# Another order for the steps of the first batch in a fused attention and gated-FFN kernel

## The chip, the cores and the metric

One NeuronCore of a Trainium2 chip runs the whole program. The metric is the device time of one execution in microseconds, the median of the runs.

## The reference

The input x has 16 batches of 512 tokens with 256 channels, float32. Each batch goes through self-attention with 16 heads of 16 channels and a causal mask, a residual and a layer norm, and then a gated FFN of hidden size 1024 with scaled weights, again with residual and layer norm:

```python
qkv = x @ Wqkv + bqkv
att = softmax(where(causal, q @ k.T * scale, -inf))
x = layernorm(x + (att @ v) @ Wout + bout)
h = silu((x @ w1.T) * s1) * ((x @ w2.T) * s2)
h = gelu((h @ h1.T) * sh1)
h = gelu((h @ h2.T) * sh2)
x = layernorm(x + (h @ w3.T) * s3)
```

## The kernel before

Each engine runs its own program, and all of them walk through the same written lists of steps, each picking out its own share of a step. `HEAD_ORDER` (line 116) is the list of the first iteration: the attention of batch 0, the first part of batch 1's attention, and the loading and testing of the FFN's weights. `FIRST_ORDER` (line 145) follows it, then `ORDER` (line 62), the loop in which one batch's attention runs beside the FFN of the batches before, and `TAIL_ORDER`. A step's name has the kind, the batch (0 or 1 in the head) and its arguments: `max:1:0:3:2` is the row maximum of batch 1, group 0, token tile 3, head 2. The 16 heads are worked in four groups of four.

The steps that matter here:

- `qk` (PE line 1170): a group's queries and keys. ACT writes the high half of the sum with the bias (line 796), DVE the low half (line 931). For batch 0 the halves lie in buffers of their own; for batch 1 they all go through the one buffer `c`, so ACT waits until the group before has been saved (line 792). SP saves the halves to DRAM in four transfers (lines 528 to 531).
- `stack`: the operands of the scores. In batch 0 PE sets them out with pick matrices (lines 1122 and 1127) and ACT copies them (lines 737 and 740). In batch 1 SP loads them in six transfers (lines 592 to 595) when the save has landed.
- `max`: PE makes scores (line 1110), DVE takes the row maximum (line 915), two banks in turn. `neg_split` (lines 923 and 925) negates a group's maxima and splits them, `neg_max` turns them on PE (line 1136), and ACT copies them into the stack (line 774). The group's exponentials wait for that.
- `exp`: PE makes the transposed scores (line 1098), ACT the exponential (line 765), GpSimd the causal mask (line 682). A group has eleven. `pv` is the product with V (line 1158), `o_out` its copy by ACT (line 816) and its move by SP (lines 616 and 617).
- `v`: a tile of V (PE line 1190, ACT line 804). `bias` is the output bias (line 1177); GpSimd adds it to the input rows, which `load_x` has SP load (lines 562 and 697).
- `raw` and `weights`: ACT issues two transfers for each of eleven pieces of the FFN's weights, DRAM to DRAM (line 744), and from there to SBUF when that has landed (line 748). `weight_test` has DVE gather the low bits of a piece (line 899), `low_bits` reduces them (line 903), and `weight_flag` (lines 906 and 1182) makes a flag of them. PE loads the flag and takes one of two copies of the rest of the program (line 1272).
- `den`, `rec_save`, `rec_load`, `den_turn`, `y`, `ln1_stats`, `ln1` and `x1_turn`: the division by the softmax's sums, the output projection, the layer norm and the turn of batch 0 for the FFN.

The order on an engine is that of the list; nothing is moved at run time. A step of which an engine has no share is skipped by it. The PSUM ring of three banks is given out by the list too (`ring_banks`, line 206): a step waits until the one before it in its bank has been read.

Of the kernel before, what the change touches and what calls it, by code (L numbers as in the profile page):

```python
# [113 lines left out]


HEAD_ORDER = """
raw:0:0 qk:0:0 qk:0:1 stack:0:0 max:0:0:3:0 table:0:Exp:0 max:0:0:3:1 stack:0:1 columns:0 raw:0:1 max:0:0:3:2
max:0:0:3:3 qk:0:2 max:0:0:2:0 max:0:0:2:1 v:0:0 raw:0:2 max:0:0:2:2 max:0:0:2:3 max:0:0:1:0 qk:0:3
max:0:0:1:1 max:0:0:1:2 stack:0:2 max:0:0:1:3 raw:0:3 max:0:0:0:0 max:0:0:0:1 stack:0:3 max:0:0:0:2
max:0:0:0:3 weights:0:0 neg_split:0:0 v:0:1 load_x:0 max:0:1:3:0 max:0:1:3:1 raw:0:4 v:0:2 max:0:1:3:2  # L120
max:0:1:3:3 neg_max:0:0 bias:0 exp:0:0:0 exp:0:0:1 max:0:1:2:0 weights:0:1 v:0:3 max:0:1:2:1 exp:0:0:2
max:0:1:2:2 exp:0:0:3 max:0:1:2:3 exp:0:0:4 max:0:1:1:0 exp:0:0:5 raw:0:5 max:0:1:1:1 exp:0:0:6 max:0:1:1:2
pv:0:0:0 weights:0:2 max:0:1:1:3 exp:0:0:7 max:0:1:0:0 exp:0:0:8 exp:0:0:9 max:0:1:0:1 max:0:1:0:2 weights:0:3
max:0:1:0:3 exp:0:0:10 raw:0:6 neg_split:0:1 max:0:2:3:0 max:0:2:3:1 neg_max:0:1 load_xT:1 pv:0:0:1
max:0:2:3:2 o_out:0:0 max:0:2:3:3 exp:0:1:0 weights:0:4 max:0:2:2:0 exp:0:1:1 max:0:2:2:1 exp:0:1:2
max:0:2:2:2 raw:0:7 exp:0:1:3 max:0:2:2:3 exp:0:1:4 max:0:2:1:0 raw:0:8 exp:0:1:5 max:0:2:1:1 exp:0:1:6
max:0:2:1:2 pv:0:1:0 max:0:2:1:3 weights:0:5 exp:0:1:7 max:0:2:0:0 exp:0:1:8 max:0:2:0:1 exp:0:1:9 max:0:2:0:2
exp:0:1:10 raw:0:9 max:0:2:0:3 neg_split:0:2 max:0:3:3:0 pv:0:1:1 o_out:0:1 qk:1:0 max:0:3:3:1 raw:0:10
neg_max:0:2 max:0:3:3:2 max:0:3:3:3 exp:0:2:0 max:0:3:2:0 stack:1:0 exp:0:2:1 weights:0:6 max:0:3:2:1
exp:0:2:2 max:0:3:2:2 exp:0:2:3 max:0:3:2:3 exp:0:2:4 max:0:3:1:0 weights:0:7 exp:0:2:5 max:0:3:1:1 exp:0:2:6  # L130
weights:0:8 max:0:3:1:2 pv:0:2:0 max:0:3:1:3 exp:0:2:7 exp:0:2:8 max:0:3:0:0 max:0:3:0:1 exp:0:2:9 max:0:3:0:2
exp:0:2:10 max:0:3:0:3 neg_split:0:3 qk:1:1 weights:0:9 weights:0:10 weight_test:0:0 neg_max:0:3 max:1:0:3:0
pv:0:2:1 o_out:0:2 stack:1:1 weight_test:0:1 weight_test:0:2 exp:0:3:0 exp:0:3:1 max:1:0:3:1 exp:0:3:2
exp:0:3:3 exp:0:3:4 weight_test:0:3 max:1:0:3:2 weight_test:0:4 exp:0:3:5 exp:0:3:6 max:1:0:3:3 pv:0:3:0
exp:0:3:7 max:1:0:2:0 exp:0:3:8 weight_test:0:5 exp:0:3:9 max:1:0:2:1 exp:0:3:10 pv:0:3:1 weight_test:0:6
o_out:0:3 den:0 max:1:0:2:2 v:1:0 v:1:1 weight_test:0:7 max:1:0:2:3 max:1:0:1:0 weight_test:0:8 max:1:0:1:1
max:1:0:1:2 max:1:0:1:3 weight_test:0:9 max:1:0:0:0 max:1:0:0:1 max:1:0:0:2 max:1:0:0:3 neg_split:1:0
weight_test:0:10 v:1:2 low_bits:0 neg_max:1:0 rec_save:0 rec_load:0 exp:1:0:0 max:1:1:3:0 exp:1:0:1
max:1:1:3:1 exp:1:0:2 max:1:1:3:2 exp:1:0:3 exp:1:0:4 max:1:1:3:3 max:1:1:2:0 exp:1:0:5 exp:1:0:6 v:1:3
exp:1:0:7 max:1:1:2:1 exp:1:0:8 max:1:1:2:2 exp:1:0:9 max:1:1:2:3 exp:1:0:10 den_turn:0 qk:1:2 y:0:0:0  # L140
max:1:1:1:0 o_out:1:0 max:1:1:1:1 y:0:0:1 y:0:1:0 y:0:1:1 ln1_stats:0 max:1:1:1:2 max:1:1:1:3 pv:1:0:1 ln1:0
stack:1:2 max:1:1:0:0 max:1:1:0:1 max:1:1:0:2 max:1:1:0:3 neg_split:1:1 x1_turn:0:0 neg_max:1:1 x1_turn:0:1
"""
# [1171 lines left out]
```

## Time and profile before

| | |
|---|---|
| median of 3 runs | 2251.17 us (2250.86 to 2251.55) |
| span of the profiled execution | 2245.9 us |
| PE busy | 2155.0 us, 96% |
| DVE busy | 1266.2 us, 56% |
| ACT busy | 1314.8 us, 59% |
| GpSimd busy | 490.6 us, 22% |
| mean granted PE clock | 0.986 of full speed |

The span runs from the first to the last instruction of the one profiled execution; that execution has no time of its own beside it, and what the runs have over it lies around the span. A line of a timeline reads: start in us, duration in us, engine, line of the kernel, operation, output and inputs, count, and in brackets the idle time before it with what ended it. SPq and ACTq are the queues on which SP and ACT issue transfers. PEld is the load of PE's stationary operand, whose time lies beside PE's.

### The profile page before, as it was taken

What the parts mean: (1) busy time and instruction counts of PE and PEld (TensorE: products, weight loads), DVE (VectorE), ACT (ScalarE), POOL (GpSimd) and SP (SyncE); (2) the same over time, 40 slices, a digit from 0 to 9 for tenths busy, and PEclk for the clock granted to TensorE, in tenths of its full rate; (3) what the DMA queues carried; (4) which work ended last, traced back from release to release, by engine and by line L of the source; (5) the groups of instructions that cost most, each with busy time, mean ns of one, the idle gap of its engine ahead of it and who ended that gap; (6) DMA issues with size and microseconds to landing.
All of it is one profiled execution on the core that took longest, in us unless ns stands there. A gap on an engine that the chain in (4) does not pass through costs nothing.

```text
span 2245.9 us, 52053 instructions
## 1 busy us (share of the span) xinstructions
PE 2155.0 (96%) x16294; PEld 1874.6 (83%) x16294; DVE 1266.2 (56%) x3928; ACT 1314.8 (59%) x2807; POOL 490.6 (22%) x899
## 2 busy tenths in 40 slices
PE   7679999999999999999999999999999999999998
PEld 4348888888888889888888888889888888888898
DVE  6664655655555565555655565565555655555452
ACT  5446565665656666565665666566565665655553
POOL 2212222221221222122221222222122221221220
PEclk9869999999999999999999999999999999999999
DMA  7823232222322223232223323223232223322100
GB/s 254 277 66 73 56 72 66 71 68 69 83 62 68 71 69 77 65 77 71 61 70 79 74 54 74 65 65 77 65 78 68 62 69 80 77 51 52 32 6 10
DMA packets 95942, 167.72 MB, mean 75 GB/s; under 512 B 19204, under 2 KB 38404, under 8 KB 95672
## 3 DMA queue, kind: packets, MB, share of 16 engines
q1 hardware_dynamic: 88152, 141.22, 25.4%
q10 hardware_dynamic: 7520, 23.07, 2.9%
q8 instruction: 149, 2.44, 0.5%
q14 instruction: 121, 0.99, 0.2%
HBM read 98.26 MB, written 68.17 MB: 74 GB/s over the span
## 4 chain that ended last, share of the span: by engine, by line
PE 65%; issue 14%; DVE 3%; ACT 3%; DMA 3%; POOL 3%; SPq 2%; ACTq 0%; DVEq 0%; POOLq 0%
PE ring L1235 35%; PE ring L1220 7%; PE pO L1158 5%; PE pS L1098 4%; PE pM L1110 4%; PE ring L1170 4%; PE ring L1248 3%; DMA qk_d<-c 2%; POOL Xlo L689 2%; PE ring L1200 1%; ACT c L796 1%; DVE c L931 1%; ACT probs_b L765 1%; DVE full_g L954 1%; DVE x1Tlo L939 1%
## 5 line engine op out<-in xcount | busy, mean ns | idle before, releaser
L915 DVE CUSTOM_DVE_ANT_0 pM<-pM,mask 128x512 f32<-128x512 f32 (+3 forms) x1024 | 494.7, 505 | 350.2 <-PE pM L1110 281.2
L1235 PE MATMUL ring<-Yhi,H 128*128 128x256 f32 x1984 | 495.3, 286 | 6.1 <-DVE c L931 5.9
L1235 PE MATMUL ring<-Xhi,H 128*128 128x256 f32 x1984 | 497.6, 290 | 0.0
L1235 PE MATMUL ring<-Ylo,H 128*128 128x256 f32 x1984 | 487.9, 282 | 0.0
L1235 PE MATMUL ring<-Xlo,H 128*128 128x256 f32 x1984 | 483.8, 283 | 0.0
L1235 PEld LDWEIGHTS ring<-Yhi,H 128*128 128x128 f32 x1984 | 378.2, 191 | 16.0 <-issue 9.5
L1235 PEld LDWEIGHTS ring<-Xhi,H 128*128 128x128 f32 x1984 | 379.0, 191 | 4.5 <-issue 3.4
L1235 PEld LDWEIGHTS ring<-Ylo,H 128*128 128x128 f32 x1984 | 379.0, 191 | 3.3
L1235 PEld LDWEIGHTS ring<-Xlo,H 128*128 128x128 f32 x1984 | 379.8, 191 | 1.1
L1110 PE MATMUL pM<-Ks,Qs 128*128 128x512 f32 x992 | 287.2, 341 | 24.9 <-DVE mx L915 12.7
L859 ACT ACTIVATE Yhi<-ring,cols 128x256 fp32r<-128x256 f32 x248 | 117.4, 474 | 292.1 <-PE ring L1235 227.6
L1098 PE MATMUL pS<-Qs,Ks 128*128 128x512 f32 x744 | 258.1, 394 | 22.6 <-ACT probs_b L765 6.9
L1220 PE MATMUL ring<-x1Thi,W 128*128 128x256 f32 x1024 | 255.1, 285 | 5.6 <-DVE full_g L954 3.8
L1220 PE MATMUL ring<-x1Tlo,W 128*128 128x256 f32 x1024 | 252.9, 282 | 0.0
L860 ACT ACTIVATE full_h<-ring,cols 128x256 f32<-128x256 f32 x512 | 239.0, 467 | 0.0
L859 ACT ACTIVATE Xhi<-ring,cols 128x256 fp32r<-128x256 f32 x248 | 117.2, 472 | 187.1 <-PE ring L1235 141.5
L1110 PEld LDWEIGHTS pM<-Ks,Qs 128*128 128x128 f32 x992 | 172.3, 192 | 49.1 <-DVE mx L915 21.7
L682 POOL TENSOR_SCALAR_AFFINE_SELECT probs_a<-probs_a 128x256 f32<-128x256 f32 x144 | 62.4, 435 | 667.6 <-ACT probs_a L765 667.1
L1220 PEld LDWEIGHTS ring<-x1Thi,W 128*128 128x128 f32 x1024 | 194.6, 190 | 12.7 <-issue 5.8
L962 DVE TENSOR_TENSOR Xlo<-full_h,Xhi 128x256 fp32r<-128x256 f32 x248 | 113.0, 456 | 157.5 <-ACT full_h L860 156.1
L1098 PEld LDWEIGHTS pS<-Qs,Ks 128*128 128x128 f32 x744 | 133.3, 191 | 78.7 <-ACT probs_b L765 27.4
L1220 PEld LDWEIGHTS ring<-x1Tlo,W 128*128 128x128 f32 x1024 | 194.8, 190 | 2.8
(148 smaller groups left out, 3554.5 us busy)
## 6 DMA issues: line engine op xcount, KB each, us to landing
qk_d<-c SPq DMA_DIRECT2D x120, 256.0 KB, 3.4
Qs<-qk_d SPq DMA_DIRECT2D x120, 192.0 KB
Ks<-qk_d SPq DMA_DIRECT2D x120, 192.0 KB
qk_d<-c SPq DMA_DIRECT2D x120, 128.0 KB, 3.1
xTs<-in_xT SPq DMA_DIRECT2D x16, 512.0 KB, 4.9
xz<-in_x SPq DMA_DIRECT2D x16, 512.0 KB, 4.0
raw<-in_h ACTq DMA_DIRECT2D x8, 1024.0 KB, 8.8
H<-raw ACTq DMA_DIRECT2D x8, 1024.0 KB, 13.6
```

The lines of the kernel that those rows point to most:

```text
L682: nc.gpsimd.affine_select(out=tri_p, in_=tri_p, compare_op=ALU.is_ge, fill=0.0, base=0, pattern=[[0, 2], [1, P]], channel_multiplier=-1).t ...
L859: nc.scalar.activation(hi, src, ACT.Gelu, scale=sc)
L860: nc.scalar.activation(full_h[:], src, ACT.Gelu, scale=sc).then_inc(h_full, 1)
L915: nc.vector.tensor_tensor_reduce(pM[:, h % 2, 0:n], pM[:, h % 2, 0:n], mask[:, T - n:T], 1.0, NEG, ALU.add, ALU.max, mx[:, t, h:h + 1]).th ...
L962: nc.vector.tensor_tensor(lo[:, j], full_h[:], hi[:, j].bitcast(F32), ALU.subtract).then_inc(h_lo, 1)
L1098: mm = nc.tensor.matmul(pS[:, nth % 2, n * wide[0]:n * (wide[-1] + 1)], K[:, p, kt * P:(kt + 1) * P], Q[:, p, first:last + 1, kt * P:T], s ...
L1110: nc.tensor.matmul(pM[:, h % 2, 0:n], Q[:, h // 2, h % 2, t * P:(t + 1) * P], K[:, h // 2, 0:n], start=True, stop=True).then_inc(m_ready, 1)
L1158: mm = nc.tensor.matmul(pO[32 * j:32 * j + VW, kt * P:T], Vo[:, kt, G * g + j], probs_of(steps, off, g, kt)[:, p, s, 0:n], start=(kt == 0) ...
L1170: mm = nc.tensor.matmul(to, Wqk[:, c, g], xTs[:, c], start=(c == 0), stop=(c == CB - 1))
L1220: mm = nc.tensor.matmul(to[:, n * HALF:(n + 1) * HALF], w, x_part, start=(c == 0 and X is x1Thi), stop=(c == CB - 1 and X is x1Tlo))
L1235: mm = nc.tensor.matmul(to, w, x_part, start=(k == 0 and m == 0), stop=(k == KB - 1 and m == 1))
L1248: mm = nc.tensor.matmul(to[:, t * C:(t + 1) * C], x_part, w, start=(k == 0 and m == 0), stop=(k == KB - 1 and m == 1))
```

## The change

The list of the first iteration is written in another order. The set of its 250 steps is the same, and so is everything outside the list. Among other moves, the input rows and the bias come earlier; the projection and stack of group 3 and three of batch 0's V tiles come behind the first group's maxima; the first two projections and stacks of batch 1 come about one group of batch 0 earlier; the weights' first pieces are issued earlier and the last two later; the first weight tests come between the last maxima of batch 0, the last ones beside the second group of batch 1; the reduction of the low bits comes near the end.

```diff
--- before.py
+++ after.py
@@ -114,32 +114,32 @@
 
 
 HEAD_ORDER = """
-raw:0:0 qk:0:0 qk:0:1 stack:0:0 max:0:0:3:0 table:0:Exp:0 max:0:0:3:1 stack:0:1 columns:0 raw:0:1 max:0:0:3:2
-max:0:0:3:3 qk:0:2 max:0:0:2:0 max:0:0:2:1 v:0:0 raw:0:2 max:0:0:2:2 max:0:0:2:3 max:0:0:1:0 qk:0:3
-max:0:0:1:1 max:0:0:1:2 stack:0:2 max:0:0:1:3 raw:0:3 max:0:0:0:0 max:0:0:0:1 stack:0:3 max:0:0:0:2
-max:0:0:0:3 weights:0:0 neg_split:0:0 v:0:1 load_x:0 max:0:1:3:0 max:0:1:3:1 raw:0:4 v:0:2 max:0:1:3:2
-max:0:1:3:3 neg_max:0:0 bias:0 exp:0:0:0 exp:0:0:1 max:0:1:2:0 weights:0:1 v:0:3 max:0:1:2:1 exp:0:0:2
-max:0:1:2:2 exp:0:0:3 max:0:1:2:3 exp:0:0:4 max:0:1:1:0 exp:0:0:5 raw:0:5 max:0:1:1:1 exp:0:0:6 max:0:1:1:2
-pv:0:0:0 weights:0:2 max:0:1:1:3 exp:0:0:7 max:0:1:0:0 exp:0:0:8 exp:0:0:9 max:0:1:0:1 max:0:1:0:2 weights:0:3
-max:0:1:0:3 exp:0:0:10 raw:0:6 neg_split:0:1 max:0:2:3:0 max:0:2:3:1 neg_max:0:1 load_xT:1 pv:0:0:1
-max:0:2:3:2 o_out:0:0 max:0:2:3:3 exp:0:1:0 weights:0:4 max:0:2:2:0 exp:0:1:1 max:0:2:2:1 exp:0:1:2
-max:0:2:2:2 raw:0:7 exp:0:1:3 max:0:2:2:3 exp:0:1:4 max:0:2:1:0 raw:0:8 exp:0:1:5 max:0:2:1:1 exp:0:1:6
-max:0:2:1:2 pv:0:1:0 max:0:2:1:3 weights:0:5 exp:0:1:7 max:0:2:0:0 exp:0:1:8 max:0:2:0:1 exp:0:1:9 max:0:2:0:2
-exp:0:1:10 raw:0:9 max:0:2:0:3 neg_split:0:2 max:0:3:3:0 pv:0:1:1 o_out:0:1 qk:1:0 max:0:3:3:1 raw:0:10
-neg_max:0:2 max:0:3:3:2 max:0:3:3:3 exp:0:2:0 max:0:3:2:0 stack:1:0 exp:0:2:1 weights:0:6 max:0:3:2:1
-exp:0:2:2 max:0:3:2:2 exp:0:2:3 max:0:3:2:3 exp:0:2:4 max:0:3:1:0 weights:0:7 exp:0:2:5 max:0:3:1:1 exp:0:2:6
-weights:0:8 max:0:3:1:2 pv:0:2:0 max:0:3:1:3 exp:0:2:7 exp:0:2:8 max:0:3:0:0 max:0:3:0:1 exp:0:2:9 max:0:3:0:2
-exp:0:2:10 max:0:3:0:3 neg_split:0:3 qk:1:1 weights:0:9 weights:0:10 weight_test:0:0 neg_max:0:3 max:1:0:3:0
-pv:0:2:1 o_out:0:2 stack:1:1 weight_test:0:1 weight_test:0:2 exp:0:3:0 exp:0:3:1 max:1:0:3:1 exp:0:3:2
-exp:0:3:3 exp:0:3:4 weight_test:0:3 max:1:0:3:2 weight_test:0:4 exp:0:3:5 exp:0:3:6 max:1:0:3:3 pv:0:3:0
-exp:0:3:7 max:1:0:2:0 exp:0:3:8 weight_test:0:5 exp:0:3:9 max:1:0:2:1 exp:0:3:10 pv:0:3:1 weight_test:0:6
-o_out:0:3 den:0 max:1:0:2:2 v:1:0 v:1:1 weight_test:0:7 max:1:0:2:3 max:1:0:1:0 weight_test:0:8 max:1:0:1:1
-max:1:0:1:2 max:1:0:1:3 weight_test:0:9 max:1:0:0:0 max:1:0:0:1 max:1:0:0:2 max:1:0:0:3 neg_split:1:0
-weight_test:0:10 v:1:2 low_bits:0 neg_max:1:0 rec_save:0 rec_load:0 exp:1:0:0 max:1:1:3:0 exp:1:0:1
-max:1:1:3:1 exp:1:0:2 max:1:1:3:2 exp:1:0:3 exp:1:0:4 max:1:1:3:3 max:1:1:2:0 exp:1:0:5 exp:1:0:6 v:1:3
-exp:1:0:7 max:1:1:2:1 exp:1:0:8 max:1:1:2:2 exp:1:0:9 max:1:1:2:3 exp:1:0:10 den_turn:0 qk:1:2 y:0:0:0
-max:1:1:1:0 o_out:1:0 max:1:1:1:1 y:0:0:1 y:0:1:0 y:0:1:1 ln1_stats:0 max:1:1:1:2 max:1:1:1:3 pv:1:0:1 ln1:0
-stack:1:2 max:1:1:0:0 max:1:1:0:1 max:1:1:0:2 max:1:1:0:3 neg_split:1:1 x1_turn:0:0 neg_max:1:1 x1_turn:0:1
+raw:0:0 qk:0:0 raw:0:1 load_x:0 qk:0:1 stack:0:0 max:0:0:3:0 max:0:0:3:1 weights:0:0 v:0:0 raw:0:2 max:0:0:3:2
+max:0:0:3:3 stack:0:1 columns:0 qk:0:2 max:0:0:2:0 max:0:0:2:1 max:0:0:2:2 max:0:0:2:3 raw:0:3 max:0:0:1:0
+stack:0:2 bias:0 max:0:0:1:1 weights:0:1 max:0:0:1:2 max:0:0:1:3 max:0:0:0:0 max:0:0:0:1 max:0:0:0:2 max:0:0:0:3
+neg_split:0:0 max:0:1:3:0 raw:0:4 neg_max:0:0 max:0:1:3:1 qk:0:3 stack:0:3 raw:0:5 max:0:1:3:2 max:0:1:3:3
+weights:0:2 max:0:1:2:0 weights:0:3 v:0:1 max:0:1:2:1 v:0:2 v:0:3 max:0:1:2:2 max:0:1:2:3 max:0:1:1:0
+max:0:1:1:1 exp:0:0:0 exp:0:0:1 max:0:1:1:2 max:0:1:1:3 exp:0:0:2 exp:0:0:3 exp:0:0:4 max:0:1:0:0 exp:0:0:5
+exp:0:0:6 exp:0:0:7 max:0:1:0:1 max:0:1:0:2 exp:0:0:8 pv:0:0:0 max:0:1:0:3 exp:0:0:9 exp:0:0:10 neg_split:0:1
+table:0:Exp:0 neg_max:0:1 raw:0:6 load_xT:1 max:0:2:3:0 max:0:2:3:1 pv:0:0:1 max:0:2:3:2 max:0:2:3:3 exp:0:1:0
+max:0:2:2:0 exp:0:1:1 max:0:2:2:1 exp:0:1:2 max:0:2:2:2 exp:0:1:3 max:0:2:2:3 exp:0:1:4 max:0:2:1:0 exp:0:1:5
+max:0:2:1:1 weights:0:4 max:0:2:1:2 o_out:0:0 max:0:2:1:3 max:0:2:0:0 exp:0:1:6 qk:1:0 raw:0:7 max:0:2:0:1
+pv:0:1:0 exp:0:1:7 exp:0:1:8 exp:0:1:9 stack:1:0 max:0:2:0:2 max:0:2:0:3 exp:0:1:10 raw:0:8 weights:0:5
+neg_split:0:2 neg_max:0:2 qk:1:1 stack:1:1 o_out:0:1 raw:0:9 pv:0:1:1 max:0:3:3:0 max:0:3:3:1 exp:0:2:0
+max:0:3:3:2 exp:0:2:1 exp:0:2:2 max:0:3:3:3 exp:0:2:3 max:0:3:2:0 exp:0:2:4 exp:0:2:5 max:0:3:2:1 weights:0:6
+max:0:3:2:2 max:0:3:2:3 exp:0:2:6 weights:0:7 max:0:3:1:0 max:0:3:1:1 max:0:3:1:2 exp:0:2:7 exp:0:2:8
+max:0:3:1:3 max:0:3:0:0 pv:0:2:0 max:0:3:0:1 exp:0:2:9 weights:0:8 max:0:3:0:2 weight_test:0:0 exp:0:2:10
+max:0:3:0:3 weight_test:0:1 raw:0:10 neg_split:0:3 neg_max:0:3 weight_test:0:2 pv:0:2:1 max:1:0:3:0 exp:0:3:0
+max:1:0:3:1 exp:0:3:1 weight_test:0:3 exp:0:3:2 exp:0:3:3 exp:0:3:4 exp:0:3:5 exp:0:3:6 o_out:0:2 max:1:0:3:2
+max:1:0:3:3 exp:0:3:7 weights:0:9 max:1:0:2:0 exp:0:3:8 exp:0:3:9 max:1:0:2:1 weight_test:0:4 max:1:0:2:2
+weight_test:0:5 pv:0:3:0 exp:0:3:10 pv:0:3:1 v:1:0 max:1:0:2:3 weight_test:0:6 max:1:0:1:0 max:1:0:1:1 o_out:0:3
+max:1:0:1:2 max:1:0:1:3 max:1:0:0:0 den:0 weights:0:10 max:1:0:0:1 weight_test:0:7 max:1:0:0:2 max:1:0:0:3
+neg_max:1:0 neg_split:1:0 rec_save:0 max:1:1:3:0 weight_test:0:8 max:1:1:3:1 max:1:1:3:2 exp:1:0:0 max:1:1:3:3
+weight_test:0:9 exp:1:0:1 exp:1:0:2 v:1:1 exp:1:0:3 exp:1:0:4 exp:1:0:5 max:1:1:2:0 rec_load:0 v:1:2 exp:1:0:6
+den_turn:0 max:1:1:2:1 max:1:1:2:2 exp:1:0:7 weight_test:0:10 exp:1:0:8 y:0:0:0 max:1:1:2:3 max:1:1:1:0 y:0:0:1
+exp:1:0:9 exp:1:0:10 qk:1:2 y:0:1:0 max:1:1:1:1 v:1:3 max:1:1:1:2 y:0:1:1 max:1:1:1:3 ln1_stats:0 pv:1:0:1
+max:1:1:0:0 max:1:1:0:1 max:1:1:0:2 max:1:1:0:3 neg_split:1:1 ln1:0 low_bits:0 o_out:1:0 neg_max:1:1 x1_turn:0:0
+stack:1:2 x1_turn:0:1
 """
 
 FIRST_ORDER = """
```

## Rows read from the trace of the kernel before

**Rows 1.** The page, part 2: PE's busy tenths in 40 slices of 56 us.

```profile
PE   7679999999999999999999999999999999999998
```

**Rows 2.** Stretches: us, busy us of each engine, granted clock, DMA share, GB/s.

```profile
60.00:80.00 20.00, 16.24 (x73) 8.71 (x73) 10.53 (x39) 9.93 (x19) 4.21 (x11) 0.74 1.04 385
...
91.00:120.00 29.00, 17.79 (x94) 9.04 (x94) 27.37 (x41) 7.80 (x15) 7.07 (x8) 0.79 0.37 110
120.00:145.00 25.00, 20.94 (x96) 13.80 (x94) 20.65 (x59) 10.04 (x20) 4.96 (x9) 0.77 0.22 60
```

**Rows 3.** Timeline at the list's end: last split, and the flag's cast.

```profile
144.86 0.19 DVE L925 SCALAR_TENSOR_TENSOR m_wide<-mx,m_wide 128x16 fp32r<-128x16 f32 x1
...
149.72 0.13 DVE L906 CAST small<-ring 1x1 int32<-1x1 f32 x1
```

**Rows 4.** Timeline of SP, PE, DVE: the second batch's first stack and first maximum.

```profile
76.19 0.36 SPq L592 DMA_DIRECT2D Qs<-qk_d  x1
...
90.68 0.79 PE L1110 MATMUL pM<-Ks,Qs 128*128 128x512 f32 x1 [9.97 <-DMA Qs<-zero_d]
...
91.64 0.70 DVE L915 CUSTOM_DVE_ANT_0 pM<-pM,mask 128x512 f32<-128x512 f32 x1 [7.56 <-issue]
```

**Rows 5.** Timeline of PE: first exponential's scores, second and third neg_max.

```profile
39.78 0.74 PE L1098 MATMUL pS<-Qs,Ks 128*128 128x512 f32 x2 [0.36 <-ACT Qs L774]
...
49.27 0.56 PE L1136 MATMUL ring<-ident,m_wide 128*98 128x128 f32 x4
...
63.98 0.48 PE L1136 MATMUL ring<-ident,m_wide 128*98 128x128 f32 x4
```

**Rows 6.** Timeline: pick products, V product, copies of maxima, halves of a projection.

```profile
32.11 1.13 PE L1122 MATMUL pS<-c,pick_q 128*114 128x512 f32 x4
...
33.08 1.09 PE L1127 MATMUL ring<-c,pick_k 128*114 128x512 f32 x4
...
34.18 1.08 PE L1190 MATMUL ring<-Wv,xTs 128*128 128x256 f32 x4
...
38.55 2.40 ACT L774 ACTIVATE Qs<-ring 2x512 fp32r<-2x512 f32 x4 [0.40 <-PE ring L1136]
...
63.95 0.69 ACT L796 ACTIVATE c<-ring,cols 128x512 fp32r<-128x512 f32 x1 [1.29 <-PE ring L1170]
...
64.67 0.75 DVE L931 SCALAR_TENSOR_TENSOR c<-ring,cols,c 128x512 fp32r<-128x512 f32 x1 [2.53 <-ACT c L796]
```

**Rows 7.** Waits of SP's queue, 0 to 155 us: total, times, longest.

```profile
SPq L426 <- DMA qk_d<-c: 7.6, 1, 7.6
```

**Rows 8.** DMA issues, 0 to 180 us: KB each, median us to landing.

```profile
qk_d<-c SPq DMA_DIRECT2D x8, 128.0 KB, 4.5
```

**Rows 9.** Timeline of DVE: first maximum of batch 0's groups 2 and 3, last one.

```profile
49.43 0.70 DVE L915 CUSTOM_DVE_ANT_0 pM<-pM,mask 128x512 f32<-128x512 f32 x1 [0.21 <-PE pM L1110]
...
61.38 0.70 DVE L915 CUSTOM_DVE_ANT_0 pM<-pM,mask 128x512 f32<-128x512 f32 x1 [0.22 <-DVE m_wide L925]
...
78.79 0.30 DVE L915 CUSTOM_DVE_ANT_0 pM<-pM,mask 128x128 f32<-128x128 f32 x1
```

**Rows 10.** Groups of instructions, 0 to 149 us: busy us, mean ns of one.

```profile
L915 DVE CUSTOM_DVE_ANT_0 pM<-pM,mask 128x512 f32<-128x512 f32 (+3 forms) x96 | 46.3, 505 | 31.3 <-issue 22.6 <-PE pM L1110 8.0 <-DVE m_wide L925 0.2
...
L899 DVE SCALAR_TENSOR_TENSOR low_bits<-H,low_bits 128x2048 int32<-128x2048 int32 x8 | 18.6, 2327 | 0.1
```

**Rows 11.** Timeline: PE's gap, ACT's long issue, a V product at low clock.

```profile
66.14 0.50 PE L1110 MATMUL pM<-Kx,Qx 128*128 128x512 f32 x1 [1.40 <-DVE mx L915]
...
67.59 3.39 ACTq L748 DMA_DIRECT2D H<-raw  x1
...
119.35 2.02 PE L1190 MATMUL ring<-Wv,xTs 128*128 128x256 f32 x4
```

**Rows 12.** Timeline of DVE: batch 1's first split, batch 0's normalization.

```profile
120.34 0.19 DVE L925 SCALAR_TENSOR_TENSOR m_wide<-mx,m_wide 128x16 fp32r<-128x16 f32 x1
...
141.64 1.38 DVE L995 TENSOR_SCALAR xz<-xz,mv,ln_s 128x256 f32<-128x256 f32 x4 [0.25 <-POOL ln_s L701]
```

## Prediction

> **What bounds the kernel now.** First the 40 slices of the page: PE is busy at 9 tenths from the fourth slice to the last but one; the first three read 7, 6 and 7 [rows 1]. Those hold the edited list, so what is gained or lost is a shift of the moment at which PE leaves it. Second, the timeline at the end of the list: the flag that decides which loop runs is cast by DVE at 149.72 us [rows 3]; all engines pass there, and from there on the program is the same in both kernels. I therefore forecast the time of that cast and carry its shift to the total one for one. Third, three stretches inside the list [rows 2]: in 60 to 80 us PE has a mean granted clock of 0.74 (between the 1.2 and 2.4 GHz levels) and DVE is busy half the time; in 91 to 120 us DVE is busy 27.37 of 29 us, so DVE is the bound there; in 120 to 145 us it is busy 20.65 of 25. Between lies the one large hole: PE stands 9.97 us until 90.68 us for the loads of the second batch's first stack [rows 4], which SP could issue only at 76.19 us. The reordering can win this hole; the question is what it costs elsewhere.
>
> The sum is made in the profiled execution, of span 2245.9 us; the median of the runs is 2251.17 us, 5.3 us more, which lie outside the span and which I leave as they are.
>
> **The change, in order of time.** "Neg_max" below is the turn of a group's negated maxima on PE, the last thing that a group's exponentials need.
>
> *First group, then the second's maxima.* The stack of group 3 and one V product (1.13 + 1.09 + 1.08 us [rows 6]) leave the stretch ahead of the first neg_max, and the bias product, of a V product's size, enters. DVE's maxima set the pace there, so of the net 2.2 us I let 1.4 come back (bounds 0 and 2.2; SP's earlier load of the input rows and POOL's bias add on them move into time in which both had nothing to do, and cost nothing): ACT's copies of the negated maxima, at 38.55 us before [rows 6], start at 37.2. Now projection and stack of group 3 stand directly behind neg_max, and make a chain through three engines: ACT's copies 2.40, ACT's high half 0.69, DVE's low half 0.75, the two pick products 1.13 + 1.09 [rows 6]: 43.3 us. Behind that PE has three V products (3 x 1.08 = 3.2) and DVE eight maxima (8 x 0.505 = 4.0 [rows 10]), which before ran beside exponentials: 50.5 us. PE idles about 1.9 us in that chain, and a gap of 1.40 us at 66.14 us stood just ahead of the stretch of low clock; at the low level a V product takes 2.02 us instead of 1.08 [rows 11]. Bounds 0 and 6 us (all of PE's work of that stretch at half speed); I take 2.0, two V products: 52.5 us is where the first exponential's matmul stands, against 39.78 [rows 5]. From there to the second neg_max it was 9.5 us (39.78 to 49.27); with one V product and eight maxima less beside it I take off 1.1 and two maxima's 1.0: 7.4 us, so **59.9 against 49.27**, 10.6 us late. Bounds: 6 (no low clock, exponentials at the 6.5 us that ACT needs for eleven) and 14.
>
> *Second group.* 49.27 to 63.98 us [rows 5], 14.7 us. The first projection of the second batch stays inside, one step of the value products leaves, two maxima enter: no difference taken, third neg_max at 74.6.
>
> *The early projections.* The first projection of the second batch now stands two thirds through the exponentials of group 1, the second right behind the next neg_max; before, a whole group of exponentials lay between the two and nobody waited. Both write the same buffer, so ACT must wait until SP's save of the first has landed; queued behind it on ACT are the copy of group 1's output and all exponentials of group 2, and on DVE the low half and all maxima of group 3. The first low half should end some 2.6 us ahead of the third neg_max, at 72.0. How long the save takes: before, from the end of the low half (64.67 + 0.75 = 65.42 [rows 6]) to the issue of the loads at 76.19 [rows 4], 10.8 us, of which SP waited 7.6 for the landing [rows 7] and used 3.2 to issue. That was with DMA full of weight pieces. In the median over the list such a transfer lands 4.5 us after its issue [rows 8]. The new list has four pieces more issued by 40 us and fewer under way here, so I take 3.2 + 4.5: landed at 79.7. ACT is free at 74.6 + 0.5 + 2.4 = 77.5. **A new wait of 2.2 us**; bounds 0, and 5.3 at the landing of before. The DMA page of the Trainium skill (DMA: Bandwidth & Descriptors, "Queues, rings and completion order") says that each DMA engine takes turns between the queues packet by packet; by that SP's save should hardly notice ACT's backlog, the wait would be at its lower end, and the sum 2.2 us lower. The 7.6 us of rows 7 against the 4.5 of rows 8 agree only in part: the backlog slows a save. With high half and low half the maxima of group 3 start at 81.1 us, against 61.38 [rows 9].
>
> *Group 3 with the first weight tests.* The nearest row is the group before, with free running exponentials: 49.43 to 61.38 us [rows 9], 12.0 us with the split of the maxima. Three weight tests of 2.33 us [rows 10] now stand in it and right behind it, 7.0 us. The second batch's first stack is issued at about 80 us; even the 14.5 us that it needed before (76.19 to 90.68) end before it is asked for, so the hole of 9.97 us is gone. On SP its second stack now stands ahead of the move of group 1's output, and waits for the second save: 81.1 + 7.7 = 88.8, and with eleven issues at 0.8 us (3.2 for four) and 4.5 us of landing the move is done near 102. ACT's copy of group 2's output needs it, but only after seven exponentials of group 3, near 104: covered by 2 us, and late by so much as the saves are later than that. **The first maximum of the second batch: 100.1 us against 91.64** [rows 4]. That is the core of this forecast: the hole is filled, but by work that the first 60 us used to hold.
>
> *Second batch, first group.* 91.64 to the split at 120.53 [rows 4, 12], 28.9 us, DVE-bound, with nine tests. Five remain: minus 4 x 2.33 makes 19.6, so 119.7. The later issue of the last two pieces costs nothing as long as they land before their tests, which stand some 15 and 25 us behind their issue.
>
> *Second batch, second group.* 120.53 to 145.05 [rows 12, 3], 24.5 us. Out go one test and the reduction over the same 2048 columns (4.7), in come three tests (7.0), and the normalization of 1.38 us [rows 12] goes behind the split: 25.4, so 145.1.
>
> *The end.* Split to cast took 4.7 us. Reduction and normalization (3.7 us) now lie in it on DVE, beside ACT's 2.40 us of copies and PE's turns; both high halves of the normalized rows now stand behind the copies, one of about 0.7 more: 5.4. **Cast at 150.5 against 149.72: 0.8 us later, 2252.0 us.**
>
> **The rivals.** About 0.2% (4.5 us) is what a measurement of this kernel can tell from no change.
>
> *Slower: the save wait and the clock.* Place: ACT's wait ahead of the second projection. If the save takes its 10.8 us again, the wait is 5.3 instead of 2.2 us (+3.1), and PE, which has only a value product to do, stands longer than the 1.40 us that preceded the low clock before [rows 11]. Then group 3 runs as it did before, 61.38 to 79.1 and 0.6 for the split [rows 9], less the 3.4 us in which ACT's queue could not issue [rows 11]: 14.9 instead of 12.0, +2.9. In sum +6.8 us: 2258 us. It decides once the landing comes more than some 9 us after the low half. For it: 7.6 us of waiting at this very save; against: fewer pieces under way.
>
> *Faster: DVE never waits after the hole.* From 81.1 us on the three groups may run at DVE's own pace: 16 x 0.505 + 0.6 + 7.0 to 96.8; 8.1 + 5 x 2.33 + 0.4 to 116.9; the 20.65 us of rows 2 + 0.9 to 138.5; 5.4 to the cast at 143.9: -5.8 us, 2245.4 us; without the low clock and the save wait 4.2 less, 2241. For it: 27.37 of 29 us busy where tests stood between maxima, so that tests give PE and ACT time to run ahead. Against: a maximum behind a test also holds PE's queue, with the exponentials behind it.
>
> *The change does not do what it says*, that is, the stack still lands late: its loads would have to take 20 us instead of 14. Not over 3 in 100, counted with the slower case.
>
> **How the numbers follow.** The forecast, within 0.2%, has 0.41: a loss of 8.5 us against a gain of the hole's size, both with bounds of several us. The faster rival has 0.27, the slower one 0.32, a little more since the early loss is a chain that can be followed step by step, while the gain needs that nothing new waits. The likeliest case alone is 2247 to 2256; 8 in 10 needs both rivals, so 2242 to 2261.
>
> **What would show it.** Right: the second neg_max at about 60 us, ACT's second projection held by a landing near 80, no wait for a zero load ahead of the second batch, its first maximum near 100, five tests ahead of its first split, cast near 150. Wrong: a second neg_max before 55 us (then the first term is mis-sized and the kernel is faster); a first maximum of the second batch after 105; or DVE below 80% busy between 100 and 145 (then the tests are badly placed and the kernel is slower).

## The result and the profile after

Five runs of the changed kernel have a median of **2261.28 us** (2258.79 to 2268.68), five of the kernel before beside them 2251.31 us: ratio **1.0046**, 95% interval 1.0030 to 1.0062. It is slower by about 10 us, where 0.8 us were forecast, in a range that ends at 2261 us.

The profiled execution took 2260.44 us, with a span of 2258.7 us. The same views as ahead of the prediction, now of the changed kernel: first the slices of the page, then stretches between the marks of the prediction.

```profile
PE   6769999999999999999999999999999999999998
```

```profile
60.00:80.00 20.00, 13.54 (x70) 6.23 (x69) 7.76 (x30) 10.18 (x19) 3.26 (x8) 0.99 0.79 265
80.00:103.20 23.20, 16.03 (x63) 9.14 (x64) 15.65 (x38) 8.16 (x15) 7.01 (x8) 0.57 1.04 305
103.20:128.80 25.60, 15.38 (x63) 8.05 (x61) 19.35 (x40) 7.18 (x14) 7.70 (x8) 0.70 0.41 126
128.80:153.40 24.60, 20.27 (x96) 13.51 (x96) 20.27 (x53) 10.50 (x20) 7.98 (x9) 0.82 0.20 57
```

Still only the first three slices and the last are below 9 tenths [rows 1]. The clock (the column behind the five engines) held to 80 us, better than in [rows 2], and then fell to a mean of 0.57 in group 3. DVE, busy 27.37 of 29 us in the second batch's first group before [rows 2], is busy 19.35 of 25.60 us there now: four tests went out, and it waits for 6.25 us.

The timeline's rows at the marks, in order of time: second neg_max, third neg_max, the second projection's high half on ACT and low half on DVE, PE's next scores, fourth neg_max, the second batch's first maximum, then its value product, V product and the maximum behind them, the splits and the flag's cast.

```profile
55.79 0.56 PE L1136 MATMUL ring<-ident,m_wide 128*98 128x128 f32 x4
...
70.92 0.56 PE L1136 MATMUL ring<-ident,m_wide 128*98 128x128 f32 x4 [1.09 <-DVE m_wide L925]
...
78.73 0.69 ACT L796 ACTIVATE c<-ring,cols 128x512 fp32r<-128x512 f32 x1 [4.72 <-DMA qk_d<-c]
...
79.45 0.75 DVE L931 SCALAR_TENSOR_TENSOR c<-ring,cols,c 128x512 fp32r<-128x512 f32 x1 [8.59 <-ACT c L796]
...
80.92 0.79 PE L1110 MATMUL pM<-Kx,Qx 128*128 128x512 f32 x1 [5.36 <-DVE mx L915]
...
98.70 0.93 PE L1136 MATMUL ring<-ident,m_wide 128*98 128x128 f32 x4 [5.29 <-DVE m_wide L925]
...
103.22 0.70 DVE L915 CUSTOM_DVE_ANT_0 pM<-pM,mask 128x512 f32<-128x512 f32 x1 [2.38 <-PE pM L1110]
...
112.39 4.34 POOL L682 TENSOR_SCALAR_AFFINE_SELECT probs_a<-probs_a 128x256 f32<-128x256 f32 x4 [2.90 <-ACT probs_a L765]
...
116.78 0.45 PE L1158 MATMUL pO<-probs_a,Vo 128*17 128x128 f32 x8 [2.14 <-POOL probs_a L682]
117.16 2.08 PE L1190 MATMUL ring<-Wv,xTs 128*128 128x256 f32 x4
...
119.73 0.57 DVE L915 CUSTOM_DVE_ANT_0 pM<-pM,mask 128x384 f32<-128x384 f32 x1 [3.64 <-issue]
...
128.56 0.19 DVE L925 SCALAR_TENSOR_TENSOR m_wide<-mx,m_wide 128x16 fp32r<-128x16 f32 x1
...
158.32 0.14 DVE L906 CAST small<-ring 1x1 int32<-1x1 f32 x1
```

The hole [rows 4] is gone, as forecast: no wait for the stack's last load (`Qs<-zero_d`) is left ahead of the second batch. In its place stand a wait of 4.72 us for the first save, 5.29 us of PE behind the two tests that now precede the split of group 3, and 3.64 us of DVE behind the value and V products. The cast is 8.6 us late (149.72 before [rows 3]); PE's first product of the loop stands 10.4 us late (164.82 against 154.40 us). From there to the end of the span the sixteen profiled executions took 2087.7 to 2099.1 us (2091.5 before, 2093.9 changed), a spread as large as the effects here: how much a kernel wins or loses is read from the ratios over all its runs, and the marks only say where.

### The profile page after: what moved, and what is told of

Read it like the earlier page. It is cut to its first block, busy times and chain, and to the rows that moved or that the text cites. A ratio compares the mean times of both kernels' runs of the same rounds, so it can differ in the third digit from the quotient of the medians.

```text
span 2258.7 us, 52053 instructions
## 1 busy us (share of the span) xinstructions
PE 2161.4 (96%) x16294; PEld 1877.5 (83%) x16294; DVE 1266.0 (56%) x3928; ACT 1316.2 (58%) x2807; POOL 498.5 (22%) x899
## 4 chain that ended last, share of the span: by engine, by line
PE 63%; issue 17%; DVE 4%; ACT 3%; POOL 3%; DMA 3%; SPq 1%; ACTq 0%; DVEq 0%; POOLq 0%
PE ring L1235 35%; PE ring L1220 6%; PE pO L1158 5%; PE pM L1110 4%; PE pS L1098 4%; PE ring L1170 4%; PE ring L1248 3%; DMA qk_d<-c 2%; POOL Xlo L689 2%; PE ring L1200 1%; DVE c L931 1%; ACT c L796 1%; ACT probs_b L765 1%; DVE full_g L954 1%; DVE x1Tlo L939 1%
## 5 line engine op out<-in xcount | busy, mean ns | idle before, releaser
L682 POOL TENSOR_SCALAR_AFFINE_SELECT probs_a<-probs_a 128x256 f32<-128x256 f32 x144 | 68.8, 480 | 681.5 <-ACT probs_a L765 681.2
```

What stands on the lines that cost most here:

```text
L682: nc.gpsimd.affine_select(out=tri_p, in_=tri_p, compare_op=ALU.is_ge, fill=0.0, base=0, pattern=[[0, 2], [1, P]], channel_multiplier=-1).t ...
```

## The experiments

The theory: the hole is worth most of its size, and the rest of the reordering takes it back, by the chain at the start, the save wait with the low clock, and tests where others wait for DVE. The rival: the hole is worth little, since what stands behind it sets the end. Each kernel ran beside the kernel before, and its ratio is to that; between two kernels compare the ratios (0.0010 is 2.25 us; their intervals are 0.0011 to 0.0022 to either side, so a difference of two ratios is uncertain by some 0.002). Times in the table are from the one profiled execution of each, in us: starts of the instructions, and of the split its end. In code lines below, the experiments' numbers are one lower than the kernel's before (their list is a line shorter); with the second buffer they are two to five higher.

| kernel | 2nd neg_max | group 3's first maximum | batch 1's first maximum | its first split | cast | ratio |
|---|---|---|---|---|---|---|
| before | 49.27 | 61.38 | 91.64 | 120.53 | 149.72 | |
| forecast | 59.9 | 81.1 | 100.1 | 119.7 | 150.5 | 1.0004 |
| changed | 55.79 | 80.12 | 103.22 | 128.75 | 158.32 | 1.0046 |
| start as before | 49.27 | 74.43 | 96.22 | 120.30 | 149.98 | 0.9994 |
| start as changed | 57.06 | 69.70 | 99.68 | 130.94 | 160.91 | 1.0037 |
| group 3's stack ahead | 52.59 | 76.91 | 100.02 | 125.47 | 154.99 | 1.0031 |
| second projection late | 56.09 | 73.80 | 102.13 | 125.53 | 155.15 | 1.0019 |
| second buffer | 62.97 | 85.29 | 106.69 | 136.91 | 166.76 | 1.0049 |
| pieces late | 55.91 | 75.43 | 96.97 | 127.42 | 157.25 | 1.0051 |
| pieces late, move first | 58.81 | 80.02 | 100.22 | 123.70 | 153.37 | 1.0006 |
| tests behind | 55.98 | 80.84 | 97.68 | 129.98 | 160.10 | 1.0064 |
| V later | 59.03 | 84.88 | 108.00 | 130.62 | 161.29 | 1.0038 |
| two tests out | 55.40 | 79.46 | 102.58 | 124.48 | 156.71 | 1.0041 |
| three repairs | 52.30 | 72.67 | 95.14 | 117.75 | 148.48 | 0.9987 |
| first projection alone | 48.73 | 62.72 | 86.14 | 117.42 | 147.39 | 0.9977 |
| and pieces late | 48.91 | 62.92 | 87.28 | 115.93 | 145.13 | 0.9958 |
| and pieces behind | 48.69 | 62.70 | 80.19 | 108.99 | 138.48 | **0.9943** |

**Which half of the list.** Two hybrids change over behind the second neg_max: before's order up to there and the new one after it, and the reverse (the diff is that of the change, cut in two).

> The kernel before's order up to the second neg_max, then the changed kernel's order for all that is left. Theory 2 (the early chain's delay is carried through): second neg_max at 49.3 instead of 55.8, all later marks 6.5 us earlier, cast near 151.8, total 6.5 us below the changed kernel. Theory 1: the pieces of weights are issued as late as before, the save of the first projection meets a full DMA and lands as late after the low half (10 to 11 us), so the wait on ACT stays at 4.7 or grows, but the start's gain is kept as well. Rival (DMA holds the saves at a fixed time): the wait grows to 8 us or more and the total comes down by less than 3 us.

> The changed kernel's order up to the second neg_max, then the order of before. Theory 2: the delay of 6.5 us is carried, cast near 156, total 6 us above the kernel before. Rival (the hole of 9.97 us ahead of the second batch takes it up, since the loads depend on DMA and the pieces are issued earlier now): hole of 2 to 5 us, cast 149 to 152, total within 2 us of the kernel before, and then the early chain costs nothing by itself.

With before's start the new order runs even with the kernel before (0.9994, 0.9983 to 1.0005); with the new start alone it is slower by 0.37% (0.25 to 0.50). So the start makes the loss, and behind it the new order neither wins nor loses, although it fills the hole (its save wait is there with before's start too, 4.5 us). Nor does the hole take up the delay of the start, as the rival had it: with the new start alone PE's wait for the loads grew from 9.97 us [rows 4] to 13.74:

```profile
98.71 0.80 PE L1109 MATMUL pM<-Ks,Qs 128*128 128x512 f32 x1 [13.74 <-DMA Qs<-zero_d]
```

**The chain at the start.** The projection and stack of group 3 go back ahead of the first maxima:

```diff
-max:0:0:1:0 ... max:0:0:0:1 ... neg_split:0:0 ... neg_max:0:0 max:0:1:3:1 qk:0:3 stack:0:3
+max:0:0:1:0 qk:0:3 ... max:0:0:0:1 stack:0:3 ... neg_split:0:0 ... neg_max:0:0 max:0:1:3:1
```

> The changed kernel with only the projection and stack of group 3 moved back ahead of the first group's last maxima. If the chain of projection, stack and V behind the first neg_max is the cause of the late exponentials, the second neg_max comes at 50 to 53 us (55.79 in the changed kernel, 49.27 before), everything behind it as much earlier, and the time is 3 to 6 us below the changed kernel. Rival: the exponentials are late because the list puts fourteen maxima of group 1 ahead of them, whatever stands there; then the second neg_max stays within 1.5 us of 55.8 and the time within 2 us of the changed kernel.

The second neg_max came 3.2 us earlier, the cast 3.3, the ratio fell by 0.0015, which by itself is within the error. PE's timeline of this run, first neg_max and first exponential's scores:

```profile
37.92 0.56 PE L1135 MATMUL ring<-ident,m_wide 128*98 128x128 f32 x4 [0.34 <-DVE m_wide L924]
...
45.38 0.63 PE L1097 MATMUL pS<-Qs,Ks 128*128 128x512 f32 x2
```

So the chain explains half of the start's 6.5 us. The other 3.3 us come behind the first neg_max, which stands here as it did before (38.03 us), while the scores stand 5.6 us later than before [rows 5]: the list has nine maxima and three V products in between. No run shows which of them cost the time.

**The save wait.** Three ways to take it away: the second projection later, a second buffer for it (its diff leaves out the waits that go with the buffer), or fewer transfers ahead of the save.

```diff
-neg_split:0:2 neg_max:0:2 qk:1:1 stack:1:1 o_out:0:1 ... exp:0:2:6 ... o_out:0:2
+neg_split:0:2 neg_max:0:2 o_out:0:1 ... exp:0:2:6 qk:1:1 ... o_out:0:2 stack:1:1
```

> The changed kernel with one thing undone: the second batch's second projection goes from behind the third neg_max to the middle of group 2's exponentials, its stack behind the copy of group 2's output. Theory 1 (the wait for the save of the first projection, 4.72 us on ACT, and the low clock after it make the loss): no wait for the save on ACT, first maximum of group 3 near 75.5 us instead of 80.1, no low clock in 80 to 90 us, flag cast near 150.5 us instead of 158.3, total 7 to 8 us below the changed kernel. Rival (the early order of the first 56 us makes it): the wait goes, but another takes its place, cast at 156 or later, total within 2 us of the changed kernel.

```diff
+            if steps is HEAD and off == 1 and g == 1:
+                return cx[:, 0]
```

> The changed kernel, its list untouched, but the second projection of the second batch is written into a buffer of batch 0 that is free by then, so ACT need not wait for the save. Theory 1: ACT's second high half follows the copies of the maxima at about 74 us, first maximum of group 3 near 75.5, PE's gap of 5.36 us gone and with it the low clock, flag cast at 151 to 153.5, total 5 to 7 us below the changed kernel. Rival: cast at 156 or later, total within 2 us of it.

```diff
-... exp:0:1:6 qk:1:0 raw:0:7 ... exp:0:1:10 raw:0:8 weights:0:5 neg_split:0:2 neg_max:0:2 qk:1:1 stack:1:1 o_out:0:1
+... exp:0:1:6 qk:1:0 ... exp:0:1:10 neg_split:0:2 neg_max:0:2 qk:1:1 stack:1:1 raw:0:7 raw:0:8 weights:0:5 o_out:0:1
```

> The changed kernel with the two first-stage transfers of pieces 7 and 8 and the second-stage transfer of piece 5 issued behind the second projection. If the backlog of weight pieces is what makes the save slow, the save of the first projection lands 6 to 8 us after its low half instead of 10.4, the wait of ACT for it falls from 4.7 to 2 or less, the first maximum of group 3 comes 2.5 to 4 us earlier, and the time is 2 to 4 us lower. Rival (the save takes turns with the pieces and its time is its own): landing still over 9.5 us after the low half, wait and time unchanged.

In all three ACT no longer waits for the save. Late, the projection made the kernel 0.27% faster than the changed one, but group 3 then ran at a clock of 0.55:

```profile
73.80:102.00 28.20, 19.42 (x69) 10.51 (x69) 16.28 (x38) 11.02 (x20) 7.01 (x8) 0.55 1.01 334
```

So the low clock of group 3 doesn't need the save wait. Where that low clock comes from stays open. The other two gained nothing (the profiled execution of the second buffer also lost 7.2 us at the start). With the pieces late the first save took much less time. SP's timeline in the changed kernel, for the first and for the second save: the last issue, and the first stack issue behind the landing:

```profile
70.15 1.37 SPq L531 DMA_DIRECT2D qk_d<-c  x1
78.81 0.35 SPq L592 DMA_DIRECT2D Qs<-qk_d  x1
...
83.90 1.30 SPq L531 DMA_DIRECT2D qk_d<-c  x1
89.44 0.31 SPq L592 DMA_DIRECT2D Qs<-qk_d  x1
```

The same with the pieces late:

```profile
70.24 0.61 SPq L530 DMA_DIRECT2D qk_d<-c  x1
74.00 0.35 SPq L591 DMA_DIRECT2D Qs<-qk_d  x1
...
79.21 0.60 SPq L530 DMA_DIRECT2D qk_d<-c  x1
90.98 0.31 SPq L591 DMA_DIRECT2D Qs<-qk_d  x1
```

From the end of the one to the start of the other it is 7.29 and 3.15 us for the first save. For the second it is 4.24 and 11.17 us: the three pieces, issued from 73.95 us on, now stood ahead of that one, so the backlog was not taken away but handed on. Group 3 began 4.7 us earlier, the second batch 6.3, and then 5.1 us went at one instruction, ACT's copy of group 2's output. ACT's timeline of this kernel:

```profile
106.31 0.60 ACT L815 ACTIVATE Osb<-pO 128x512 f32<-128x512 f32 x1 [5.12 <-DMA den_d<-Osb]
```

And SP's, the second stack's first issue, the move and its last part:

```profile
90.98 0.31 SPq L591 DMA_DIRECT2D Qs<-qk_d  x1
...
94.46 2.48 SPq L615 DMA_DIRECT2D Oc<-Osb  x4
96.99 0.55 SPq L616 DMA_DIRECT2D den_d<-Osb  x1
```

It waits for the move of group 1's output, which stands on SP behind the second stack, which waits for the second save. With the second buffer the same copy stood 4.89 us. In the changed kernel this copy did not wait for the move; here the cover "by 2 us" of the prediction is gone. The next kernel has the late pieces and the move first:

```diff
-qk:1:1 stack:1:1 raw:0:7 raw:0:8 weights:0:5 o_out:0:1
+qk:1:1 raw:0:7 raw:0:8 weights:0:5 o_out:0:1 stack:1:1
```

> The changed kernel with the three transfers of weight pieces behind the second projection, and the move of group 1's output ahead of the second stack on SP. With the pieces alone the save wait went (group 3 began 4.7 us earlier) but the copy of group 2's output then stood 5.1 us for that move. If that is what took the gain back, the wait is gone here, the first split of the second batch stands at 121 to 124 us (128.75 changed, 127.4 with the pieces alone), the cast at 151 to 153, and the time 4 to 7 us below the changed kernel. Rival: something else holds that stretch at its length: split at 126 or later, time within 2 us of the changed kernel.

The wait is gone. The cast stands 5.0 us earlier than in the changed kernel although this execution lost 3.0 at the start, and the ratio fell by 0.0045 against the late pieces alone and by 0.0040, or 9 us, against the changed kernel: more than was expected. The second save still took 10.5 us (84.33 to 94.85 us), but ACT's copy no longer stands behind it. So the save wait and SP's order were worth taking away together: with the first alone gone, the second shows. The move first by itself was not run.

**What sets the second batch's first group.** The prediction's 19.6 us took 25.5. Three kernels move its tests or its V product.

```diff
-... weight_test:0:0 exp:0:2:10 max:0:3:0:3 weight_test:0:1 ... neg_max:0:3 weight_test:0:2 ... max:1:0:3:1
+... exp:0:2:10 max:0:3:0:3 ... neg_max:0:3 ... max:1:0:3:1 weight_test:0:0 weight_test:0:1 weight_test:0:2
```

> The changed kernel with the first three weight tests moved behind the second maximum of the second batch, where the kernel before had them. If the two tests ahead of the split of group 3 hold PE (5.29 us in the changed kernel), that wait falls below 1.5 us, the fourth neg_max and the first maximum of the second batch come 4 to 5 us earlier (103.2 to 98.5), the first split of the second batch gives back up to 7 us of tests less the 5 us in which DVE idled there, and the time is 2 to 4 us below the changed kernel. Rival: DVE is the bound behind it, so the tests cost the same there: time within 1 us, or later.

The second batch began 5.5 us earlier and its first group then took 32.3 instead of 25.5 us: here the rival was right, and the kernel was if anything slower. The three tests hold the next maxima on DVE, and PE's scores wait for those:

```profile
109.17 0.69 PE L1109 MATMUL pM<-Ks,Qs 128*128 128x384 f32 x1 [6.94 <-DVE mx L914]
```

DVE is idle as long as in the changed kernel, 6.25 us of 32.30 against 6.23 of 25.53: the three tests (7.0 us) came through nearly whole. The tests ahead of the split are no mistake.

```diff
-... pv:0:3:1 v:1:0 max:1:0:2:3 ... exp:1:0:2 v:1:1
+... pv:0:3:1 max:1:0:2:3 ... exp:1:0:2 v:1:0 v:1:1
```

> The changed kernel with the first V product of the second batch moved from the first group's maxima into its exponentials. The prediction gave that stretch DVE's pace (19.6 us); it took 25.5, with DVE idle 3.64 us behind the value product and this V product at the low clock. If PE's chain there is on the path, the split comes 1.5 to 2.5 us earlier (near 126.7), and the V product's 2 us come back in the exponentials only in part: time 0 to 2 us lower. Rival: DVE sets the pace and the idle time is only moved: split within 0.7 us, time unchanged.

```diff
-... max:1:0:2:1 weight_test max:1:0:2:2 weight_test pv:0:3:0 ... max:1:1:3:0 ... max:1:1:3:2
+... max:1:0:2:1 max:1:0:2:2 pv:0:3:0 ... max:1:1:3:0 weight_test ... max:1:1:3:2 weight_test
```

(The tests are numbered anew in this one, since they run in order.)

> The changed kernel with two of the five weight tests of the second batch's first group (those beside group 3's last exponentials and masks) taken into its second group. If DVE's load sets the pace, as the prediction had it, that stretch falls by the two tests' 4.7 us, 25.5 to 20.8, and the second one grows by as much: time unchanged. If PE's chain of masks, value product and V product sets it, DVE only waits longer there: the stretch falls by 1 to 2.5 us, by what the masks no longer lose beside the tests, and the second group grows by 4 to 5: cast 2 to 3 us later, the time 2 to 3 us over the changed kernel.

Without the V product the group took 22.6 us, and the next one 25.8 instead of 24.7 (its split stands late in the table because this execution lost 3.2 us at the start); the ratio's fall by 0.0008 is within the error. Without the two tests it took 21.9 and the next one 27.3; the time is unchanged. Neither theory's number came: DVE's load had 4.7 us to give, and 3.6 came. Part of that is the clock. Two other kernels with the same steps in this stretch as the changed one, the second projection late and the move first, took 23.4 and 23.5 us for it, at a clock of 0.86; the changed kernel had 0.70 there, the run without the tests 0.81. The timeline tells the two apart. GpSimd, PE and DVE of the run without the two tests:

```profile
111.75 0.90 POOL L681 TENSOR_SCALAR_AFFINE_SELECT probs_a<-probs_a 128x256 f32<-128x256 f32 x2 [3.09 <-ACT probs_a L764]
113.83 0.41 PE L1157 MATMUL pO<-probs_a,Vo 128*17 128x128 f32 x8 [0.48 <-POOL probs_a L681]
114.17 1.13 PE L1189 MATMUL ring<-Wv,xTs 128*128 128x256 f32 x4
115.65 0.57 DVE L914 CUSTOM_DVE_ANT_0 pM<-pM,mask 128x384 f32<-128x384 f32 x1 [4.73 <-issue]
```

A mask takes 0.45 us here, and 1.1 in the mean in the changed kernel, where two tests ran beside four of them (4.34 us for four). The masks start 9.17 us behind the first maximum in both. PE waits 0.48 instead of 2.14 us for the last mask; in the two kernels at 0.86 it waits 2.14 and 2.15, so this part is the tests'. The V product takes 1.13 instead of 2.08 us; it takes 1.13 in those two as well, so this part is the clock's. DVE still stands, 4.73 us instead of 3.64. So DVE's load does not set this stretch alone. Its waits for the chain of masks, value product, V product and next scores add to its load; tests beside the masks lengthen that chain by way of the masks, and tests ahead of maxima hold PE by way of the maxima.

**The repairs together**, on the changed kernel (chain back, pieces late, move first, V product later):

> The changed kernel with all three: the projection and stack of group 3 back ahead of the first maxima, the pieces and the move as above, the V product later. If the terms add, 3.3 us for the chain, 4 to 7 for the save wait and 1 to 2 for the V product: cast at 146 to 150 us (158.3 changed), the time 8 to 11 us below the changed kernel, so at or a little below before. Rival: they overlap, since each only uncovers the next wait: gain under 6 us, the time over before.

The ratio is 0.9987 (0.9972 to 1.0002), 0.0059 or 13 us below the changed kernel's, and even with the kernel before, since the interval holds 1. The ratios' falls one by one were 0.0015, 0.0040 and 0.0008, in sum 0.0063: as far as errors of some 0.002 each can tell, they add.

**The hole by itself**, on the kernel before:

```diff
-... exp:0:1:6 ... exp:0:1:9 ... pv:0:1:1 o_out:0:1 qk:1:0 ... max:0:3:2:0 stack:1:0
+... exp:0:1:6 qk:1:0 ... exp:0:1:9 stack:1:0 ... pv:0:1:1 o_out:0:1 ... max:0:3:2:0
```

> The order of before, with only the first projection and stack of the second batch moved one group earlier (behind exponentials 6 and 9 of group 1). If the hole is worth its size once nothing else is moved, the save lands near 69 us, the loads near 83, the wait for them ahead of the second batch (9.97 us before) falls to 2 or less, the first maximum of the second batch stands at 82 to 85 us (91.64 before), the cast at 141 to 144, and the time is 6 to 9 us below before. Rival: what the hole gives is lost again behind it, since the tests and the low clock set the pace there: first maximum earlier, but the cast at 147 or later and the time within 3 us of before.

The ratio is 0.9977 (0.9965 to 0.9989): the early projection alone is worth 5 us, less than the 6 to 9 expected, and the cast stands at the 147 us of the rival. PE's timeline shows what it left:

```profile
85.17 0.80 PE L1109 MATMUL pM<-Ks,Qs 128*128 128x512 f32 x1 [5.16 <-DMA Qs<-zero_d]
```

The last of these loads was issued at 72.73 us and took 0.63, so the landing took 11.8 us. Two kernels more move pieces 5 to 10 back as well.

```diff
-raw:0:7 ... raw:0:8 ... weights:0:5 ... exp:0:1:10 raw:0:9 ... raw:0:10 ... weights:0:6 ... weights:0:7 ... exp:0:2:6 weights:0:8 ... exp:0:2:10 ... qk:1:1 weights:0:9 weights:0:10
+exp:0:1:10 raw:0:7 raw:0:8 weights:0:5 ... exp:0:2:6 raw:0:9 raw:0:10 weights:0:6 ... exp:0:2:10 weights:0:7 weights:0:8 ... qk:1:1 ... exp:0:3:4 weights:0:9 weights:0:10
```

> The order of before with the early first projection and stack, and with the transfers of the weight pieces 5 to 10 issued later (7, 8 and the second transfer of 5 behind the exponentials of group 1, the rest in and behind group 2). If the 5.2 us that the second batch still waited with the early projection alone (its loads took 11.8 us from the last issue) are the backlog of pieces, the loads land within 6 us, the wait goes, the first maximum of the second batch stands at 80 to 82 us instead of 86.1, and the time is 3 to 5 us below that kernel, 8 to 10 below before. Rival: the pieces are then late for their tests, or the tests set the end: first split of the second batch unchanged near 117, time within 2 us of that kernel.

The timeline of the first (ACT's queue, ACT, PE) shows no late load but an issue that held ACT's exponentials, and PE's scores behind them:

```profile
72.05 5.90 ACTq L747 DMA_DIRECT2D H<-raw  x1
78.06 0.49 ACT L764 ACTIVATE probs_b<-pS 128x384 f32<-128x384 f32 x1 [6.79 <-issue]
78.60 0.79 PE L1097 MATMUL pS<-Qx,Kx 128*128 128x512 f32 x1 [5.15 <-ACT probs_b L764]
```

Its ratio is 0.9958 (0.9942 to 0.9975). The second puts no transfer among group 2's exponentials:

```diff
-exp:0:2:6 raw:0:9 raw:0:10 weights:0:6 ... exp:0:2:10 weights:0:7 weights:0:8 ... exp:0:3:4 weights:0:9 weights:0:10
+exp:0:2:6 ... exp:0:2:10 raw:0:9 raw:0:10 ... exp:0:3:1 weights:0:6 ... exp:0:3:4 weights:0:7 weights:0:8 ... exp:0:3:8 weights:0:9 weights:0:10
```

> As the run with the early projection and the late pieces, but the transfers of pieces 6 and 9, 10 that stood among group 2's exponentials (one issue took ACT 5.90 us there, with the exponentials and through them PE and DVE behind it) now behind that group. If that issue is what kept the second batch's first maximum at 87.3 us although its loads were no longer late, it stands at 82 to 84 us here, the cast at 140 to 143 (145.1), the time 2 to 5 us below that kernel. Rival: the issue stalls wherever it stands, since the transfers themselves are the limit, and then holds the next group: cast at 144 or later, time within 2 us.

Its first maximum of the second batch stands at 80.19 us, its ratio is **0.9943** (0.9921 to 0.9965), 2238.04 us against 2250.24 beside it: faster than both kernels, although PE still waits 3.24 us for the loads. With the pieces out of its way the hole was worth its size. The two steps by the pieces, 0.0019 and 0.0015, are each within the error, and clear of it only together; late pieces without the early projection were not run.

## Why the prediction was right or wrong

The forecast was wrong: a time even with before was expected, and the kernel is 10 us slower. The forecast cast was 150.5 us, the measured one 158.3. The difference of 7.8 us by the prediction's steps:

- *First group and chain*, second neg_max at 59.9: it came at 55.79, **4.1 us early**. Half of that was there ahead of the chain: ACT's copies started at 35.05 us, for 37.2. The term let 1.4 us come back, of 2.2 us of PE's products; with the projection and stack of group 3 put back the first neg_max came 3.5 us later (37.92 against 34.45), beyond the bounds of 0 and 2.2. The chain is there (half by half to 40.2, picks behind), but from the copies to the first exponential's scores (48.58) it took 13.5 us, for 15.3: at the high clock from 40 us on (1.00 in 40 to 60 us), where 2.0 us of low clock had been charged. Of nine profiled executions with this same start the mark lies at 55.4 to 57.1 in six and at 58.8, 59.0 and 63.0 in three, where the clock was low longer (0.50 from 35 to 50 us in the last): inside the bounds given.
- *Second group*: 15.1 us, for 14.7.
- *The early projections*: from third neg_max to group 3's first maximum 9.2 us, for 6.5. The step that failed is "fewer under way here": the save landed 10.4 us after its low half, as before (10.8), not 7.7, and ACT waited 4.72 us, near the bound of 5.3. Late pieces made it go, so it was the backlog: 7.29 us to the landing with it, 3.15 without. The Trainium skill (DMA: Bandwidth & Descriptors, "Queues, rings and completion order") says that each DMA engine takes turns between the queues packet by packet. The prediction reckoned that by this the save should hardly notice the backlog, and did not follow it; the runs bear that doubt out, by the 7.29 and 3.15 us.
- *Group 3 with the first tests*: 23.1 us, for 19.0. Not counted at all was PE's part behind the split: neg_max, value products and scores make 4.5 us from neg_max to the first maximum (98.70 to 103.22), where only the third test's 2.3 had been put. That is 2.2 of the 4.1 us. The rest came with the clock of 0.57, the slower rival's mechanism: it asked +3.1 for the wait and +2.9 for the clock, and got 2.7 and some 1.9. But its link from wait to clock was not shown: without the wait the clock was 0.55 in one run, and 0.76 with 21.5 us in another.
- *Second batch, first group*: 25.5 us, for 19.6. **This is the largest wrong term.** "DVE-bound, minus 4 x 2.33" took a busy share of 27.37 of 29 us [rows 2] for a pace that would hold when a third of the load goes. The load came as forecast, 19.30 us. The waits did not stay: from first maximum to split DVE was idle 1.06 of 28.89 us before, and 6.23 of 25.53 now, for the chain of masks, value product and V product. Some 2 us of that come with the clock, since the same steps took 23.4 and 23.5 us at 0.86.
- *Second group and end*: 24.7 for 25.4 and 4.9 for 5.4 us, right.
- *Behind the cast*: taken as equal, but PE's first product of the loop came 6.5 us after it, 4.7 before. In fourteen of the fifteen other profiles this took 4.6 to 5.2 us (6.75 with the tests behind); what held it here waited for nothing that the profile shows, and stays open.

So the core of the forecast was right, and its mechanism was measured: the hole is filled, by work that the start lost. What failed are the waits: the steps between the second neg_max and the cast were 11.9 us short in sum, and that the start came 4.1 us early, which hid a third of it, is luck. The slower rival came nearest (2258 us), by its save wait and its clock. Its chance of 0.32 looks too low now, since the largest terms that failed were those where a wait was to be covered or to stay small (the save, PE behind the split, DVE). The cover of 2 us for the move on SP held in the changed kernel and failed only where the save wait was taken away. The faster rival, DVE never waiting behind the hole, was wrong: it waits 6.25 of 25.60 us there. Of the signs of being wrong one came: DVE is busy 33.44 of the 45 us from 100 to 145 us, 74% (39.77, 88%, before). That the tests are then badly placed is borne out in part only: three of them moved behind cost no less, and two moved into the next group left the time unchanged.

## What to carry to other kernels

A busy share of 94% says how little an engine waits under this load and order. When a third of the load goes, the load falls as reckoned, but the waits need not stay small: price the next chain, and add what the engine waits for it. A transfer that is moved earlier lands only as early as the queue ahead of it allows; move what is not urgent out of its way, not in front of the next urgent one, and not between instructions that others wait for. Where a wait is taken away and nothing is won, look for the wait that a queue's order kept behind it, and take both away in one run before calling the cause wrong.
